# A decoder layer and a perceiver layer on one core: new instruction orders, PSUM banks and lags between units

## The reference

```python
# layer 0, 16 heads of 16
h = layernorm(x);  x = x + attention(h @ wq, h @ wk, h @ wv, ltor_mask) @ w_ao          # "self"
h = layernorm(x);  x = x + attention(h @ w_q, enc @ w_k, enc @ w_v, cross_mask) @ w_co  # "cross"
h = layernorm(x);  x = x + gelu(h @ w1) @ w2                                            # "mlp0"
# layer 1, x are the latents
q = x @ q_w;  k, v = concat([ctx, x]) @ kv_w                                            # "ctx" and "lat"
y = softmax(q k^T / 16, masked) v @ out_w + x
out = gelu(rmsnorm(y) @ w1 ) @ w2 + x                                                   # "mlp1"
# attention(): softmax(scores * mask - 10000 * (1 - mask)) @ v
```

## Time and profile before

| what | value |
|---|---|
| median of 3 runs | 1120.4 us (1119.05 to 1125.32) |
| the profiled execution's own time | 1117.1 us |
| its span, first to last instruction | 1115.1 us |
| PE busy | 1037.7 us, 93% of the span, 19304 matmuls |
| PEld busy | 908.9 us, 82% |
| DVE busy | 982.0 us, 88%, 2360 instructions |
| ACT busy | 785.7 us, 70% |
| POOL busy | 633.9 us, 57% |
| mean granted clock of TensorE | 0.991 |

### The profile page before, as it was taken

How to read it: one execution, slowest core, us unless ns; L and a number is a source line. 1 busy time by engine, 2 the same in 40 slices (tenths; PEclk the granted TensorE clock), 3 DMA queues, 4 the chain that set the end, 5 groups by cost and what they waited for, 6 DMA issues and landing times.

```text
span 1115.1 us, 46381 instructions
## 1 busy us (share of the span) xinstructions
PE 1037.7 (93%) x19304; PEld 908.9 (82%) x19304; DVE 982.0 (88%) x2360; ACT 785.7 (70%) x1773; POOL 633.9 (57%) x903
## 2 busy tenths in 40 slices
PE   6677899999999999999999999999999999999997
PEld 5666678888888888888888888888888888878786
DVE  3888979989989999899999989999999999889774
ACT  2446677877667777777677777766777777666786
POOL 3866666555556565655565656555665566464421
PEclk9898999999999999999999999999999999999999
DMA  9541111122111121221111111111111122110111
GB/s 316 175 146 47 46 28 29 33 43 43 38 34 35 39 37 34 43 43 36 33 38 37 39 34 43 43 33 31 43 33 34 43 43 43 32 28 17 26 30 31
DMA packets 117473, 55.09 MB, mean 49 GB/s; under 512 B 98960, under 2 KB 115088, under 8 KB 116240
## 3 DMA queue, kind: packets, MB, share of 16 engines
q1 hardware_dynamic: 117264, 52.13, 19.4%
HBM read 26.93 MB, written 4.19 MB: 28 GB/s over the span
## 4 chain that ended last, share of the span: by engine, by line
PE 45%; DVE 23%; DMA 12%; ACT 10%; issue 6%; POOL 2%; SPq 1%; ACTq 0%; POOLq 0%; DVEq 0%
PE psum L469 11%; PE psum L649 10%; PE psum L609 7%; PE psum L482 6%; DMA turned_lat<-pair_lat 5%; PE psum L595 5%; DMA turned_cross<-pair_cross 4%; PE psum L576 4%; ACT staging L1867 2%; ACT hid_mlp L1867 2%; DVE prob_self L1214 2%; DVE prob_cross L1243 2%; PE psum L455 2%; DVE mx_ctx L1224 2%; DVE prob_cross L1214 1%
## 5 line engine op out<-in xcount | busy, mean ns | idle before, releaser
L2270 POOL TENSOR_TENSOR prob_self<-prob_self,add_self 128x512 f32<-128x512 f32 x64 | 90.9, 1437 | 87.8 <-DVE prob_self L1214 87.7
L2270 POOL TENSOR_TENSOR prob_cross<-prob_cross,add_cross 128x512 f32<-128x512 f32 x64 | 81.1, 1288 | 59.9 <-DVE prob_cross L1214 59.9
L2219 POOL TENSOR_TENSOR rstd_mlp<-var_mlp,minus_half 128x1 f32<-128x1 f32 x64 | 36.3, 567 | 123.1 <-DVE var_mlp L1137 89.8
L1867 ACT ACTIVATE hid_mlp<-psum,folded,undo_in 128x128 f32<-128x128 f32 x256 | 95.8, 464 | 7.2 <-PE psum L469 7.2
L1867 ACT ACTIVATE staging<-psum,cols,undo_in 128x128 f32<-128x128 f32 x256 | 96.2, 457 | 4.9 <-PE psum L469 3.9
L649 PE MATMUL psum<-hi_n,staging 128*128 128x256 f16 x512 | 94.3, 273 | 1.2 <-DVE staging L1276 1.2
L469 PE MATMUL psum<-turned_mlp,hi_m 128*128 128x128 f16 x1024 | 92.7, 219 | 2.4 <-DMA turned_mlp<-pair_mlp 2.1
L469 PE MATMUL psum<-turned_mlp,hi_n 128*128 128x128 f16 x1024 | 92.5, 219 | 0.3 <-DMA turned_mlp<-pair_mlp 0.3
L649 PE MATMUL psum<-hi_m,parts_mlp 128*128 128x256 f16 x512 | 90.1, 273 | 1.1 <-DVE parts_mlp L1276 1.1
L469 PE MATMUL psum<-turned_mlp,lo_n 128*128 128x128 f16 x512 | 88.9, 219 | 0.0
L469 PE MATMUL psum<-turned_mlp,lo_m 128*128 128x128 f16 x512 | 88.9, 219 | 0.0
(11 more groups left out here) (267 smaller groups left out, 3801.5 us busy)
## 6 DMA issues: line engine op xcount, KB each, us to landing
xin<-in_x SPq DMA_DIRECT2D x32, 128.0 KB, 2.3
late<-in_ctxT SPq DMA_DIRECT2D x4, 1024.0 KB, 7.6
ctxT<-in_ctxT SPq DMA_DIRECT2D x32, 128.0 KB, 2.1
late<-in_x SPq DMA_DIRECT2D x4, 1024.0 KB, 6.2
out<-xb SPq DMA_DIRECT2D x32, 128.0 KB, 1.9
staging<-in_w_m SPq DMA_DIRECT2D x2, 1024.0 KB, 7.2
staging<-in_w_n SPq DMA_DIRECT2D x2, 1024.0 KB, 5.2
mask<-in_mask_cross SPq DMA_DIRECT2D x32, 32.0 KB, 1.9
```

Source lines behind the costliest of these rows:

```text
L1867: last = e.activation(hid[t][g][:, j * P:(j + 1) * P], ps[:, j * P:(j + 1) * P], ACT.Gelu_apprx_tanh, bias=b1[:, 4 * g + j:4 * g + j + 1], ...
L2219: e.tensor_tensor(rstd[t][:, :], var[t][:, :], minus_half[:, :], ALU.pow).then_inc(sem["rstd_" + t], 1)
L2270: e.tensor_tensor(ch, ch, over_heads(a[:, :]), ALU.add).then_inc(sem["added_" + t], 1)
```

## The change

The set of operations is the same call for call on every engine, with the same buffers and waits, except that prob_turn also waits for the identity (once, met at the start). What differs is the order of the calls on all five engines, in prologue, loop and epilogue, the PSUM banks, and the lags: FILL is 7, so that the loop has 25 passes and the prologue fills one slot more. In the loop k_cross (t-2 for t-1), k_ctx (t-4 for t-3), q_lat (t-4 for t-3), the end of the cross attention (t-3 for t-2), prob_turn(self) and its exponential (t-2 for t-1) and outward(mlp1) (t-7 for t-6) lag one pass more; on SyncE the transposes of self are issued at t-1 for t, those of mlp1 at t-6 for t-5, the store at t-8 for t-7. The loops, the first old and new lines of the prologue of SyncE, and the two other edits:

```diff
-FILL, SLOTS = 6, UNITS
+FILL, SLOTS = 7, UNITS
...
             def prob_turn(u, t, b):
 
+                q.wait_ge("constants", IDENT)
                 q.wait_ge("shifted_" + t, 2 * u + 2)
...
 @block.tensor
...
 for t in range(FILL, SLOTS):
-    mix(t - 2, "self", 4)
-    score_bank(t - 4, "ctx", 0)
-    score(t - 4, "ctx", 6)
-    heads_turn(t - 5, "lat", 5)
-    heads_turn(t - 2, "self", 4)
-    v_lat(t - 4, 2)
+    prob_turn_bank(t - 2, "self", 1)
+    heads_turn(t - 3, "cross", 6)
+    k_ctx(t - 4, 3)
+    v_lat(t - 4, 0)
+    prob_turn(t - 2, "self", 7)
+    project(t - 3, "cross", 5)
+    q_lat(t - 4, 6)
+    mix(t - 2, "self", 2)
+    k_cross(t - 2, 5)
+    heads_turn(t - 5, "lat", 7)
+    heads_turn(t - 2, "self", 6)
     hidden(t - 6, "mlp1", 0, 1)
-    project(t - 2, "self", 7)
-    project(t - 5, "lat", 5)
-    k_lat(t - 4, 6)
-    hidden(t - 6, "mlp1", 1, 7)
-    score_bank(t - 4, "lat", 0)
-    hidden(t - 3, "mlp0", 0, 2)
-    score(t - 4, "lat", 4)
-    hidden(t - 3, "mlp0", 1, 6)
-    qk_self(t - 1, 3)
-    q_cross(t - 2, 0)
-    prob_turn_bank(t - 4, "lat", 2)
-    v_self(t - 1, 4)
-    prob_turn(t - 4, "lat", 5)
-    score_bank(t - 2, "cross", 6)
+    project(t - 2, "self", 2)
+    k_lat(t - 4, 0)
+    score_bank(t - 4, "ctx", 6)
+    score(t - 4, "ctx", 4)
+    project(t - 5, "lat", 2)
+    hidden(t - 6, "mlp1", 1, 3)
+    score_bank(t - 4, "lat", 6)
+    score(t - 4, "lat", 0)
+    hidden(t - 3, "mlp0", 0, 4)
+    hidden(t - 3, "mlp0", 1, 5)
+    v_self(t - 1, 3)
+    outward(t - 7, "mlp1", 0, 2)
+    q_cross(t - 2, 6)
+    outward(t - 7, "mlp1", 1, 2)
+    score_bank(t - 2, "cross", 4)
     score(t - 2, "cross", 0)
-    outward(t - 3, "mlp0", 0, 3)
-    outward(t - 3, "mlp0", 1, 3)
-    prob_turn_bank(t - 4, "ctx", 6)
+    qk_self(t - 1, 6)
+    prob_turn_bank(t - 4, "ctx", 3)
     prob_turn(t - 4, "ctx", 7)
+    prob_turn_bank(t - 4, "lat", 0)
+    prob_turn(t - 4, "lat", 1)
+    outward(t - 3, "mlp0", 0, 4)
+    outward(t - 3, "mlp0", 1, 4)
     score_bank(t - 1, "self", 0)
-    k_ctx(t - 3, 5)
-    score(t - 1, "self", 2)
-    mix(t - 4, "lat", 6)
-    prob_turn_bank(t - 2, "cross", 7)
-    prob_turn(t - 2, "cross", 4)
-    v_cross(t - 1, 1)
+    score(t - 1, "self", 6)
+    prob_turn_bank(t - 2, "cross", 3)
+    prob_turn(t - 2, "cross", 5)
+    mix(t - 4, "lat", 4)
+    mix(t - 2, "cross", 3)
+    v_cross(t - 1, 0)
     v_ctx(t - 3, 2)
-    mix(t - 2, "cross", 5)
-    outward(t - 6, "mlp1", 0, 3)
-    q_lat(t - 3, 0)
-    heads_turn(t - 2, "cross", 7)
-    outward(t - 6, "mlp1", 1, 3)
-    prob_turn_bank(t - 1, "self", 4)
-    prob_turn(t - 1, "self", 1)
-    project(t - 2, "cross", 5)
-    k_cross(t - 1, 3)
...
 @block.vector
...
 for t in range(FILL, SLOTS):
+    shifted(t - 2, "self", 0)
+    shifted(t - 2, "self", 1)
+    heads_low(t - 3, "cross")
+    divided(t - 5, "lat")
+    hidden_lo(t - 7, "mlp1", 0)
+    k_spread(t - 4, "ctx", 0)
+    add_residual(t - 3, "cross")
     moments(t - 3, "mlp0")
-    k_spread(t - 2, "cross", 0)
+    q_bias_lat(t - 4)
     denominators(t - 2, "self")
     divided(t - 2, "self")
+    k_spread(t - 2, "cross", 0)
+    hidden_lo(t - 7, "mlp1", 1)
+    heads_low(t - 2, "self")
+    low_pair(t - 3, "mlp0")
+    k_spread(t - 4, "ctx", 1)
+    k_spread(t - 2, "cross", 1)
+    add_residual(t - 2, "self")
+    moments(t - 2, "cross")
+    low_pair(t - 1, "self")
+    k_spread(t - 4, "lat", 0)
+    k_spread(t - 4, "lat", 1)
     masked(t - 4, "ctx", 0)
     masked(t - 4, "ctx", 1)
-    heads_low(t - 2, "self")
-    low_pair(t - 3, "mlp0")
+    low_pair(t - 2, "cross")
+    add_residual(t - 5, "lat")
     largest_score(t - 4, "ctx", 0)
-    add_residual(t - 2, "self")
-    moments(t - 2, "cross")
-    k_spread(t - 2, "cross", 1)
-    largest_score(t - 4, "ctx", 1)
-    k_spread(t - 4, "lat", 0)
-    add_residual(t - 5, "lat")
-    k_spread(t - 4, "lat", 1)
     moments(t - 5, "mlp1")
-    low_pair(t - 2, "cross")
     largest_score(t - 4, "lat", 0)
     largest_score(t - 4, "lat", 1)
     largest_both(t - 4, 0)
+    largest_score(t - 4, "ctx", 1)
+    shifted(t - 4, "lat", 0)
     largest_both(t - 4, 1)
-    shifted(t - 4, "lat", 0)
+    hidden_lo(t - 3, "mlp0", 0)
     shifted(t - 4, "lat", 1)
-    hidden_lo(t - 3, "mlp0", 0)
-    q_bias_self(t - 1)
     q_bias_cross(t - 2)
-    k_spread(t - 1, "self", 0)
-    k_spread(t - 1, "self", 1)
+    moments(t, "self")
     hidden_lo(t - 3, "mlp0", 1)
     masked(t - 2, "cross", 0)
     masked(t - 2, "cross", 1)
-    moments(t, "self")
+    k_spread(t - 1, "self", 0)
+    q_bias_self(t - 1)
     largest_score(t - 2, "cross", 0)
-    add_mlp(t - 3, "mlp0")
+    k_spread(t - 1, "self", 1)
     shifted(t - 2, "cross", 0)
     largest_score(t - 2, "cross", 1)
-    hidden_lo(t - 6, "mlp1", 0)
     shifted(t - 2, "cross", 1)
+    add_mlp(t - 3, "mlp0")
     masked(t - 1, "self", 0)
+    lat_low(t - 3)
+    masked(t - 1, "self", 1)
     low_pair(t - 5, "mlp1")
-    k_spread(t - 3, "ctx", 0)
-    masked(t - 1, "self", 1)
-    lat_low(t - 3)
-    k_spread(t - 3, "ctx", 1)
     largest_score(t - 1, "self", 0)
-    shifted(t - 1, "self", 0)
-    largest_score(t - 1, "self", 1)
+    add_mlp(t - 7, "mlp1")
+    denominators(t - 4, "lat")
     denominators(t - 2, "cross")
     divided(t - 2, "cross")
-    hidden_lo(t - 6, "mlp1", 1)
-    denominators(t - 4, "lat")
-    shifted(t - 1, "self", 1)
-    heads_low(t - 2, "cross")
-    q_bias_lat(t - 3)
-    divided(t - 4, "lat")
-    low_pair(t, "self")
-    add_mlp(t - 6, "mlp1")
-    add_residual(t - 2, "cross")
+    largest_score(t - 1, "self", 1)
...
 @block.scalar
...
 for t in range(FILL, SLOTS):
-    heads_out(t - 5, "lat")
+    heads_out(t - 3, "cross")
+    values(t - 4, "ctx")
+    exponential(t - 2, "self", 0)
+    exponential(t - 2, "self", 1)
+    values(t - 4, "lat")
     normalize(t - 3, "mlp0")
     heads_out(t - 2, "self")
+    heads_out(t - 5, "lat")
     gelu(t - 6, "mlp1", 0)
-    values(t - 4, "lat")
     normalize(t - 2, "cross")
-    hidden_hi(t - 6, "mlp1", 0)
     gelu(t - 6, "mlp1", 1)
     gelu(t - 3, "mlp0", 0)
+    scaled_high(t - 5)
     hidden_hi(t - 3, "mlp0", 0)
     gelu(t - 3, "mlp0", 1)
-    scaled_high(t - 5)
+    hidden_hi(t - 6, "mlp1", 0)
     hidden_hi(t - 3, "mlp0", 1)
-    exponential(t - 4, "lat", 0)
-    exponential(t - 4, "lat", 1)
     values(t - 1, "self")
     exponential(t - 4, "ctx", 0)
     exponential(t - 4, "ctx", 1)
+    exponential(t - 4, "lat", 0)
+    exponential(t - 4, "lat", 1)
     lat_high(t - 3)
     exponential(t - 2, "cross", 0)
     exponential(t - 2, "cross", 1)
+    normalize(t, "self")
     hidden_hi(t - 6, "mlp1", 1)
     values(t - 1, "cross")
-    heads_out(t - 2, "cross")
-    normalize(t, "self")
-    exponential(t - 1, "self", 0)
-    exponential(t - 1, "self", 1)
-    values(t - 3, "ctx")
...
 @block.gpsimd
...
 for t in range(FILL, SLOTS):
+    high_pair(t - 1, "self")
     root(t - 3, "mlp0")
-    mask_add(t - 1)
-    plus_bias(t - 1, "self")
+    plus_bias(t - 6, "mlp1")
+    mask_add(t - 2)
     high_pair(t - 3, "mlp0")
-    plus_bias(t - 6, "mlp1")
     root(t - 2, "cross")
-    plus_bias(t - 3, "mlp0")
     high_pair(t - 2, "cross")
     ctx_high(t - 1)
-    plus_bias(t - 2, "cross")
+    mask_keys(t - 3)
+    plus_bias(t - 3, "mlp0")
     root(t - 5, "mlp1")
     shifted_ctx(t - 4, 0)
-    mask_keys(t - 2)
+    plus_bias(t - 2, "cross")
     shifted_ctx(t - 4, 1)
     ctx_low(t - 1)
     added(t - 2, "cross", 0)
     added(t - 2, "cross", 1)
+    root(t, "self")
     added(t - 1, "self", 0)
     added(t - 1, "self", 1)
-    plus_bias(t - 3, "lat")
-    root(t, "self")
-    high_pair(t, "self")
+    plus_bias(t - 4, "lat")
+    plus_bias(t, "self")
...
 @block.sync
...
 for t in range(FILL, SLOTS):
     load_x(t)
+    across(t - 6, "mlp1")
     across(t - 3, "mlp0")
+    store(t - 8)
+    across(t - 1, "self")
+    across(t - 2, "cross")
+    across(t - 3, "lat")
     load_rest(t)
-    across(t - 2, "cross")
-    store(t - 7)
-    across(t - 3, "lat")
-    across(t - 5, "mlp1")
-    across(t, "self")
...
```

```diff
             load_x(0)
             load_weight(0, "qkv")
             load_columns(0)
+            load_x(1)
+            load_part(0, "ctx", 0)
             load_weight(0, "q")
-            load_part(0, "ctx", 0)
+            load_tile(0, "out")
+            load_mask(0)
+            across(0, "self")
+            load_tile(0, "side")
+            load_x(2)
             load_rows(0)
-            load_tile(0, "side")
-            load_mask(0)
-            load_x(1)
-            load_tile(0, "out")
             load_part(0, "ctx", 1)
-            load_x(2)
-            across(0, "self")
-            load_part(0, "ctx", 2)
             load_weight(0, "m1")
...
```

More of the change, by code:

```diff
@@ new lines, in _ @@
+            prob_turn(3, "self", 7)
+            score_bank(4, "self", 6)
+            score(4, "self", 0)
+            mix(3, "self", 2)
+            prob_turn(1, "cross", 5)
+            hidden(0, "mlp0", 0, 6)
```

(103 more changed lines are left out.)

1380 lines of the change are left out of this document (718 added, 662 removed).

## The result

The changed kernel takes 1104.67 us in the median of 4 runs (1101.72 to 1106.6), the kernel before 1120.28 (1119.05 to 1125.32, 4 runs beside them): a ratio of 0.985, 95% interval 0.9813 to 0.9887. The profiled execution of the changed kernel took 1106.6 us, its span is 1104.8; so the spans differ by 10.3 us and the medians by 15.6. The range, 1075 to 1109, holds it; the forecast of 1088 was too low by 16.7.

A forecast was written before the change was run, and what follows sets the result against it. TensorE's list was taken to bound each loop pass at 31.0 us, with late transposes above it. The sum 1117.1 - 28.2 + 2.5 - 3 - 1 = 1087.4 gave a forecast of 1088 us, range 1075 to 1109.

The forecast's parts named there:

- The bound of the loop: Loop: TensorE's own list bounds a pass at 31.0 us; VectorE has 1.45 us to spare.
- the 28.2 us: Loop: late lat and cross transposes cost 28.2 us, all expected gone, between -20 and -31.6.
- The margins: Loop, transpose issue to first use: lat about 4.5 us (was 2.8), cross 5.0 (was 2.7), against worst landing 4.6.
- The rival in which the landings grow later: Loop: nothing gained, waits move elsewhere or closer transposes on SyncE land later; 1120 us, chance 0.06.
- The seams: Loop, ScalarE at pass start and VectorE's masked(ctx): little air, 0.1 us a pass each counted, +2.5 us (0 to +12).
- The rivals of costly seams: Loop: seams cost half a microsecond a pass, 1098 us, chance 0.13; or VectorE or ScalarE becomes bound, 1139, chance 0.06.
- The rule on the table load: ScalarE seam: skill's 1380 ns drain would push gelu 1.4 us later; rows show none, so the sum omits it.
- The median: Whole run: median was 3.3 us above the profiled execution; that part should mostly vanish, giving 1088.
- Prologue and epilogue: Fill and drain: -3 us (-8 to +8) for the prologue, -1 us (-4 to +4) for the epilogue.
- It costs no more there than here if the fill and the drain keep their density: Prologue and epilogue: the pass leaving the loop costs about its own 31 us of TensorE's work there.
- the forecast's own 1079 to 1097: Total time: the range of the main forecast without its rivals, given chance 0.67.
- The clock there was 0.94; I leave its share as it is: Prologue: granted clock of 0.94 taken as unchanged, with no term in the sum.

The follow-up runs named there:

- the clock kept: Changed kernel with 64 matmuls of 128x512 halves, results unread, added into free banks at five TensorE waits of the fill: 1098.17 us, ratio 0.9818.
- the low half first too: Changed kernel with GpSimd's first context low half moved directly behind its high half, 50 matmuls added in the fill, and the old drain: 1093.44 us, ratio 0.9792.
- Three moves on two engines: Kernel before with TensorE's q(lat) later, VectorE's cross low halves before the mlp1 moments, and VectorE's q(lat) bias three stages later: 1109.45 us, ratio 0.9914.

## Why the prediction was right, and where it was wrong

- **The bound of the loop** was read rightly. 31.01 us against 31.03 measured; the whole of the 28.2 us went (834.5 - 26 x 31.03 = 27.7).
- **The margins** were counted rightly: 4.5 for lat is 4.5 in the row above, for a landing of 4.5. All lat transposes of the loop land before their first user, four of them by less than 0.3 us. For cross it is 4.47, where 5.0 was counted; that it sufficed is luck in part, since the latest of the loop took 4.2 us and lat's took 4.5. The rival in which the landings grow later came true in the medians, and the new air covered it.
- **The seams**: 2.5 us expected, 25 x 0.02 = 0.5 found. The 6.8 us of weight-load waits for shifted(self), 0.3 at most, are what shows of the chain across the pass's end, and the 4.4 us at q(cross) are a seam that was not foreseen. The rivals of costly seams are out.
- **The rule on the table load** (the Trainium skill, ScalarE: Activation LUTs, What ACT_TABLE_LOAD costs) gave 1380 ns of drain behind each load; it did not show, and the trace decides against the page here: the changed kernel's groups have 35 and 34 loads of 1283 ns, with 0.6 us idle before all of each group (two loads more than before, as foreseen), and a pass of 31.03 us leaves no sign of 1.4 us more.
- **The median**: it was to stand near the sum for the profiled execution, and does (1104.67 and 1106.6).
- **Prologue and epilogue: the step that failed.** "It costs no more there than here if the fill and the drain keep their density": they did not. On the prediction's own split (the whole moved pass in the fill) the prologue came to +7.0 instead of -3, at the edge of its bounds, and the epilogue to +10.5 instead of -1, far out of them. Part of that is a wrong split, 6.5 us of the pass's work being in the drain; together the two ends are 17.5 us instead of -4, and that is the miss. Nor did the pass cost 31 us there: it cost 48.5. That the stated range still holds the result is luck: its upper end was put there for costly seams, which did not come, and the time lies outside the forecast's own 1079 to 1097.
- **"The clock there was 0.94; I leave its share as it is"** is the term that was never priced. It was 0.87 (and the 0.94 itself leaves out the first 23 us, which ran at the lower level). With the clock kept, the first full pass starts 5.6 to 7.4 us earlier; with the low half first too, at 192.41, where the prediction had 193. The earlier loads and transposes it counted did come (the first q and k start at 15.77 instead of 21.08), but behind them stood one GpSimd order with 8.85 us in it, and "the other waits of the fill are reordered in ways that no row prices" was true and no reason for -3 as the likeliest value.
- What stays open: the 4.0 us of the drain, which the order of before in its place did not bring back, and some 3 us of the fill.
- The experiments on the loop show that the time was not to be had cheaply. The late landings were read as TensorE's matter. But VectorE's list is 1.45 us shorter than TensorE's in a pass, and a stage moved on one engine alone moved the wait to the other and made every pass slower, also those that had lost nothing: 32.35 us a pass from the second one on in place of 32.02. Three moves on two engines got 0.9 of a per cent. The changed lists, in which all engines agree, got the pass to within 0.02 us of the 31.01 of a pass that waits for no transpose.

## What to carry to other kernels

Where two engines are both near the bound, a stage can't be moved on one of them alone: look up who waits for it and move that too, or count its new wait in every pass against the late cases cured. Price the fill and the drain by their own rows, and look at the granted clock there before trusting that work moved into them costs what it did in the loop; matmuls into free banks at waits that come early, and whose followers others wait for, can be worth more than they cost (64 of them were here; 6 alone showed nothing in the total). Before anything else, read the two or three longest waits of a fill: one line of order on an engine far from the bound brought the first full pass forward by 4 us here, of which 2 show in the total.

## What the runs showed of the hardware

- The lower clock followed short waits too. In the changed kernel TensorE had 1.65 us without work before 26.46 us, the clock was 0.50 from 30 to 35, and 32 matmuls took 387 ns each instead of 276. With 6 matmuls in that wait it stayed at 1.00 to 40 us. It is not the length of the one wait alone: the kernel before has 2.09 us without a matmul before 31.60 us and is granted 1.00 up to 46.9.
- At the start the lower level held longer than the granted clock says: 305 ns for a matmul at 17.57 us in the kernel before, 218 at 17.76 in the changed one, whose records begin there. A mean clock over a fill has to be read with the durations beside it.
- Why transposes land late was open in the prediction. The DMA records of the changed kernel hold 153 packets of 16 KB for instructions, each of which takes 1.1 us, about one every 7 us. Of the 123 transposes from 205 to 975 us, 81 have such a packet between their issue and 2.6 us after it; these take 3.26 us on the mean to land, and 60% of them more than 2.9. The other 42 take 2.51, and 5% of them more than 2.9. In the kernel before it is the same (69 of 120 with 3.18 us, 51 with 2.45). This is a coincidence in two traces, found afterwards; no run took the fetches away.

```profile
q8 instruction: 153, 2.51, 0.9%
```

- GpSimd's stages took longer than usual while VectorE split weights into halves (side from 44.29, m1 from 48.76 us): the bias addition of 128x512 took 2.23 and 2.30 us there, against a mean of 1.28 for the cross activations in the whole run (below). No run took the splits away.

```profile
L2401 POOL TENSOR_TENSOR prob_cross<-prob_cross,add_cross 128x512 f32<-128x512 f32 x64 | 80.7, 1279 | 57.3 <-DVE prob_cross L1258 57.3
```
